# Rotary tables renewed by half sequence, weights in three turns, inverse norms on 128x32, and a new order of the slots

## The reference, cut to what matters

```
q, k, v = split(shift_tokens(x) @ Wqkv)           # 16 heads of 64
q = l2norm(q) * q_scale;  k = l2norm(k) * k_scale
q = q*cos*scale + rotate_half(q)*sin*scale        # k with 1/scale
o = softmax(q @ k.T * 8 over this and the previous window of 32) @ v
x = x + o @ Wo
xn = layernorm(shift_tokens(x)) * ln_g + ln_b     # the rows are shifted here too
a, gate = split(xn @ W1 + b1)
x = x + (a * gelu(gate)) @ W2 + b2
```

## Time and profile before

| | |
|---|---|
| median of three runs | 2486.25 us (2473.58, 2486.25, 2487.25) |
| the profiled execution | 2478.85 us, of which the span of its instructions 2477.0 |
| mean granted TensorE clock | 0.952 of full speed |
| PE, PEld | 2240.8 us busy (90%), 1255.8 (51%) |
| DVE | 1696.9 (69%) |
| POOL | 1463.3 (59%) |
| ACT | 1281.8 (52%) |
| DMA | 208.27 MB, mean 84 GB/s; queue of SP 32.4% of 16 engines |
| first and last norms of a front (L704) | 554.8 and 2369.8 us |

### The profile page before, as it was taken

One profiled execution on the slowest core, in us unless ns is written; L12 is line 12 of the kernel. 1 busy time (PEld: TensorE's weight loads), 2 busy tenths in 40 slices (PEclk: granted clock), 3 DMA queues, 4 the chain that ended last, 5 costly groups with the idle time before them and its releaser, 6 DMA issues. The chain is left out here.

```text
span 2477.0 us, 60119 instructions
## 1 busy us (share of the span) xinstructions
PE 2240.8 (90%) x23184; PEld 1255.8 (51%) x23184; DVE 1696.9 (69%) x3412; ACT 1281.8 (52%) x2402; POOL 1463.3 (59%) x1342
## 2 busy tenths in 40 slices
PE   8999999976889899998999989999899998999985
PEld 4545455533445455554555545555455554555542
DVE  5556555546767678776787767877668776787752
ACT  5565565632454455544555445554455544565442
POOL 3344433336666677666776667766666676676740
PEclk9999999987999999999999999999999999999997
DMA  1000000023343533445334353344534435344330
GB/s 56 6 1 5 1 5 1 1 65 96 90 114 99 145 89 97 114 100 143 88 96 114 101 143 89 96 113 102 143 88 105 112 93 143 95 101 110 93 86 21
DMA packets 219577, 208.27 MB, mean 84 GB/s; under 512 B 44194, under 2 KB 211104, under 8 KB 217760
## 3 DMA queue, kind: packets, MB, share of 16 engines
q1 hardware_dynamic: 219296, 204.45, 32.4%
HBM read 83.79 MB, written 13.63 MB: 39 GB/s over the span
## 5 line engine op out<-in xcount | busy, mean ns | idle before, releaser
L722 POOL TENSOR_TENSOR T<-T,RB 128x512 f32<-128x512 f32 x384 | 487.1, 1300 | 264.7 <-DMA RB<-norms 264.7
L647 PE MATMUL bank<-XT,WQK 128*128 128x256 f32 x1536 | 460.4, 426 | 155.6 <-DVE T L668 131.7
L673 POOL TENSOR_TENSOR T<-T 128x512 f32<-128x512 f32 x384 | 503.4, 1317 | 127.5 <-DVE T L668 127.4
L756 PE MATMUL bank<-WU,XT 128*32 128x512 f32 x3072 | 431.7, 635 | 1.7 <-ACT U L763 1.6
L647 PEld LDWEIGHTS bank<-XT,WQK 128*128 128x128 f32 x1536 | 278.1, 201 | 250.6 <-DVE T L668 151.7
L653 ACT ACTIVATE SQ<-bank 128x512 f32<-128x512 f32 x384 | 227.7, 593 | 296.0 <-PE bank L647 295.3
L413 POOL TENSOR_SCALAR PR<-PR,RI 128x512 f32<-128x512 f32 x256 | 173.9, 692 | 314.4 <-DVE RI L354 314.4
L763 ACT ACTIVATE U<-bank 128x512 f32<-128x512 f32 x384 | 229.3, 597 | 178.7 <-PE bank L853 140.3
L667 DVE TENSOR_TENSOR T<-bank,TAB 128x512 f32<-128x512 f32 x384 | 260.9, 679 | 83.0 <-ACT SQ L653 47.7
L349 DVE CUSTOM_DVE_ANT_0 PR<-bank,causal 128x512 f32<-128x512 f32 x256 | 174.3, 682 | 201.4 <-PE bank L192 201.3
L818 POOL TENSOR_TENSOR PL<-PL,RIL 128x512 f32<-128x512 f32 x192 | 201.3, 1048 | 143.9 <-DVE RIL L811 143.9
(11 more groups left out here) (110 smaller groups left out, 3463.3 us busy)
## 6 DMA issues: line engine op xcount, KB each, us to landing
RB<-norms SPq DMA_DIRECT2D x384, 128.0 KB, 3.1
KZ<-T SPq DMA_DIRECT2D x384, 128.0 KB, 2.6
QP<-T SPq DMA_DIRECT2D x192, 256.0 KB, 4.3
TAB<-rotary_dram SPq DMA_DIRECT2D x12, 1024.0 KB, 8.2
norms<-RN SPq DMA_DIRECT2D x96, 128.0 KB, 2.5
WQK<-wqk_halves_dram SPq DMA_DIRECT2D x12, 512.0 KB, 6.0
WVS<-wv_turned_dram SPq DMA_DIRECT2D x30, 128.0 KB, 2.5
WOS<-wo_lanes_dram SPq DMA_DIRECT2D x30, 128.0 KB, 2.7
```

What stands on the lines that cost most here:

```text
L647: m = pe.matmul(b[:, ab * HALF:(ab + 1) * HALF], WQK[:, kind, i, ab, :], XT[s % 2][:, hf * HALF:(hf + 1) * HALF], start=True, stop=True)
L673: pool.tensor_tensor(t1, t1, T2[i % 2][:, ::-1, :], ALU.add).then_inc(l_rotated.sem, 1)
L722: pool.tensor_tensor(t1, t1, RB[:, i:i + 1, :].to_broadcast([P, 2, HALF]), ALU.mult).then_inc(l_scaled.sem, 1)
L756: i = pe.matmul(bank[1][h * WIN:(h + 1) * WIN, :], XT[s % 2][:, c0:c0 + WIN], WU[:, lp * HG + h, :], start=True, stop=True)
```

## The change

- **Tables and weights.** WQK becomes three buffers of one kind each, taken in turn, so that the next layer's weights are loaded while the present ones are in use. The table is renewed in four parts (half sequence and kind), each as soon as the last products with that part are done, and folded in four parts by POOL.
- **Norms on 128x32.** ScalarE copies the square sums from PSUM to SS. SP gathers the meaningful rows by four DMAs into SM, 128x32, where every number counts. Clamp, guess and Newton step run on 128x32, and the store in DRAM is 16 KB for 128 KB. Norms in still reads four times into RB. `sp_norms` is cut in two, `sp_norms_out` and `sp_norms_in`.
- **Feed-forward rows** are scaled by ScalarE as rstd x + (-mean rstd); VectorE makes -mean and POOL the product.
- **Order.** All five slots are rewritten. In SP's slot the gather comes first, then the relayout; weight load, `sp_next_vo` and `sp_ffn_weights` stand between relayout and norms out; table load and `sp_shift` between norms out and norms in. On TensorE `values(k+1, 1)` stands late in slot k rather than early in the next, and `turn_probs` of half 0 at the slot's end. On POOL the four scalings stand first in the slot and the rotations of the next fronts behind them. On VectorE clamp and Newton step of a front are two entries with a product between them.

```diff
-            WQK = sbl('WQK', [P, 2, HG, 2, P])
+            WQK = [sbl(f'WQK{i}', [P, HG, 2, P]) for i in range(3)]
...
-            SM = sbl('SM', [P, HALF])
-            LG = sbl('LG', [P, HALF])
-            Y0 = sbl('Y0', [P, HALF])
-            Y2 = sbl('Y2', [P, HALF])
-            RN = sbl('RN', [P, HALF])
+            SS = sbl('SS', [P, HALF])
+            SM = sbl('SM', [P, WIN])
+            LG = sbl('LG', [P, WIN])
+            Y0 = sbl('Y0', [P, WIN])
+            Y2 = sbl('Y2', [P, WIN])
+            RN = sbl('RN', [P, WIN])
+            negm = sbl('negm', [P, TPB])
+            nmr = sbl('nmr', [P, TPB])
...
-            def sp_load_front(l, kind):
-                last = (l - 1) * 4 * BATCH + 14 + kind
+            def sp_load_weights(l, kind):
+                n = 2 * l + kind
+                if n >= 3:
+                    sp.wait_ge(l_front_done.sem, l_front_done.at((n - 3) // 2 * 16 + 14 + (n - 3) % 2))
+                sp.dma_start(WQK[n % 3][:, :, :, :], wqk[l, :, kind, :, :, :]).then_inc(s_wk[n % 3], 16)
+
+            def sp_load_table(l, part):
+                hf, kind = divmod(part, 2)
+                cols = slice(hf * HALF, (hf + 1) * HALF)
                 if l:
-                    sp.wait_ge(l_front_done.sem, l_front_done.at(last))
-                    sp.wait_ge(l_products.sem, l_products.at(last))
-                sp.dma_start(WQK[:, kind, :, :, :], wqk[l, :, kind, :, :, :]).then_inc(s_wk[kind], 16)
-                sp.dma_start(TAB[:, kind, :, :, :], rot[kind]).then_inc(s_wk[kind], 16)
-
-            def pool_fold_scale(l, kind):
-                pool.wait_ge(s_wk[kind], 32 * (l + 1))
+                    sp.wait_ge(l_products.sem, l_products.at((l - 1) * 16 + 12 + part))
+                sp.dma_start(TAB[:, kind, :, :, cols], rot[kind, :, :, :, cols]).then_inc(s_tb[part], 16)
+
+            def pool_fold_scale(l, part):
+                hf, kind = divmod(part, 2)
+                cols = slice(hf * HALF, (hf + 1) * HALF)
+                pool.wait_ge(s_tb[part], 16 * (l + 1))
                 for ab in range(2):
                     c = l * 4 + kind * 2 + ab
-                    i = pool.tensor_scalar(TAB[:, kind, :, ab, :], TAB[:, kind, :, ab, :], QSC[:, c:c + 1], 1.0, ALU.mult, ALU.mult)
+                    i = pool.tensor_scalar(TAB[:, kind, :, ab, cols], TAB[:, kind, :, ab, cols], QSC[:, c:c + 1], 1.0, ALU.mult, ALU.mult)
                 i.then_inc(l_folded.sem, 1)
...
-                pe.wait_ge(l_clamped.sem, l_clamped.at(f - 1))
+                pe.wait_ge(l_sums_kept.sem, l_sums_kept.at(f - 1))
...
+            def act_keep_sums(f):
+                act.wait_ge(l_sums_done.sem, l_sums_done.at(f))
+                act.wait_ge(s_sc, 64 * f)
+                act.activation(SS[:, :], bank[4][:, 0:HALF], ACT.Copy).then_inc(l_sums_kept.sem, 1)
+
+            def sp_gather_sums(f):
+                sp.wait_ge(l_sums_kept.sem, l_sums_kept.at(f))
+                sp.wait_ge(l_newton.sem, l_newton.at(f - 1))
+                for j in range(HG):
+                    r = slice(j * WIN, (j + 1) * WIN)
+                    sp.dma_start(SM[r, :], SS[j * WIN:j * WIN + HG, :].rearrange('h (t c) -> h t c', c=WIN)).then_inc(s_sc, 16)
+
             def dve_clamp(f):
-                dve.wait_ge(l_sums_done.sem, l_sums_done.at(f))
-                dve.wait_ge(l_newton.sem, l_newton.at(f - 1))
-                dve.wait_ge(l_guess.sem, l_guess.at(f - 1))
-                dve.tensor_scalar(SM[:, :], bank[4][:, 0:HALF], FAR, NORM2_EPS, ALU.min, ALU.max).then_inc(l_clamped.sem, 1)
+                dve.wait_ge(s_sc, 64 * (f + 1))
+                dve.tensor_scalar(SM[:, :], SM[:, :], FAR, NORM2_EPS, ALU.min, ALU.max).then_inc(l_clamped.sem, 1)
...
-            def sp_norms(f):
+            def sp_norms_out(f):
                 sp.wait_ge(l_newton.sem, l_newton.at(f))
                 if f >= 2:
                     sp.wait_ge(s_rb, 64 * (f - 1))
                 sp.dma_start(norms[f % 2], RN[:, :]).then_inc(s_rn, 16)
+
+            def sp_norms_in(f):
                 sp.wait_ge(s_rn, 16 * (f + 1))
                 sp.wait_ge(l_scaled.sem, l_scaled.at(f - 1))
-                rows = norms[f % 2].rearrange('(g h) (a c) -> h a g c', h=WIN, a=1)
+                rows = norms[f % 2].rearrange('(g h t a) c -> h a g (t c)', h=HG, t=8, a=1)
                 for h in range(HG):
                     sp.dma_start(RB[h * WIN:(h + 1) * WIN, :, :], rows[h].to_broadcast([WIN, HG, HALF])).then_inc(s_rb, 16)
...
+                dve.tensor_scalar(negm[:, :], mv[:, :, 0], -1.0, None, ALU.mult)
...
-            def dve_ffn_scale(s):
-                dve.wait_ge(f_rstd_done.sem, f_rstd_done.at(s))
-                dve.wait_ge(f_turned.sem, f_turned.at(s - 1))
+                pool.wait_ge(f_rstd_done.sem, f_rstd_done.at(s, 0))
+                pool.tensor_tensor(nmr[:, :], negm[:, :], rstd[:, :], ALU.mult).then_inc(f_rstd_done.sem, 1)
+
+            def act_ffn_scale(s):
+                act.wait_ge(f_rstd_done.sem, f_rstd_done.at(s))
+                act.wait_ge(f_turned.sem, f_turned.at(s - 1))
                 for t in range(TPB):
-                    i = dve.tensor_scalar(XN2[:, t, :], X2S[:, t, :], mv[:, t, 0:1], rstd[:, t:t + 1], ALU.subtract, ALU.mult)
+                    i = act.activation(XN2[:, t, :], X2S[:, t, :], ACT.Identity, scale=rstd[:, t:t + 1], bias=nmr[:, t:t + 1])
                 i.then_inc(f_scaled.sem, 1)
...
-            def change_at(v):
-                return v % 16 < 2 and 0 < v // 16 < DEPTH
+            def change_at(v, n):
+                return v % 16 < n and 0 < v // 16 < DEPTH
...
```

240 lines of the change are left out of this document (110 added, 130 removed).

## The result

| | before | after |
|---|---|---|
| median | 2483.38 us (2473.58 to 2487.25, 4 runs) | 2570.07 us (2568.90 to 2571.97, 4 runs) |
| ratio | | 1.0356, 95% interval 1.0323 to 1.0389 |
| profiled execution, span | 2478.85, 2477.0 | 2568.9, 2567.1 |
| granted TensorE clock | 0.952 | 0.953 |
| first and last norms in | 556.9, 2378.6 | 556.6, 2474.4 |

The change makes the kernel 3.6% slower, 87 us. The forecast was 2622 us, within 2530 to 2740. All of the loss lies between the first norms in and the last, 1821.7 us before and 1917.9 after (+96.2); what comes behind the last one takes 92.7 us for 98.4. In what follows a **round** is the time from the start of norms in of one front to that of the next.

A forecast was written before the change was run, and what follows sets the result against it. The SP-DMA-POOL loop was taken as the bound. From 2478.9 us, +5.3 us a step over 23 steps (+122) and +21 for layer changes gave 2622 us, range 2530 to 2740.

The forecast's parts named there:

- the loop: SP, DMA and POOL: norms in, RB lands, POOL scales, relayout, norms out lands, next norms in; about 18.5 us a round.
- shift ahead of norms in: SP queue, K front: a wait of 1.85 us becomes the shift's 8.1 us, +6.3 us a step.
- its old place: Shift behind norms in, in the kernel before: removing its cost, less later RB landing, gives -0.4 us a step.
- POOL late behind it: K front after the shift: POOL's scaling, late from VectorE's stall, is late no more, -0.5 us a step.
- `sp_next_vo`: SP queue, Q front: its two issues and 256 KB now stand ahead of norms out, +0.8 us a step.
- small norms: Norms out of 16 KB for 128 KB lands sooner: -0.3 us in three fronts, -0.9 us a step.
- The other steps: Layer changes, with weights, tables and feed-forward weights issued around norms out, plus the first layer's loads: +21 us in all.
- rival 3: SP queue: the gather comes into the loop and late sums hold the relayout; 2718 us or past 2900; chance 0.12.
- Row scaling on ScalarE: Feed-forward row scaling moved from VectorE into ScalarE's gaps, outside the loop: price 0.
- The gather: SP queue, beside RB's landing and POOL's scaling: four to five us of slack, so 0; upper bound about 1 us a front.
- Rival 1: VectorE's wait for X2S, not the loop, sets the period, so the change is faster: 2296 us; chance 0.10.
- Rival 2: The shift mostly hides, its third issue holding SP 1 us for 6.4: about 2490 us, no change; chance 0.08.

The follow-up runs named there:

- b_shift_between: Kernel before, with only the three X2S shift copies moved between norms out and norms in: 2586.95 us, ratio 1.0404 to the kernel before.
- a_shift_split: Changed kernel with the 127-partition shift copy cut into 112 and 15, its place kept: 2456.73 us, ratio 0.9880 to the kernel before.
- a_loads_behind: Changed kernel with next_vo, feed-forward weights, layer weights and table parts issued behind norms in, shift left in place: 2493.86 us, ratio 1.0042 to the kernel before.
- b_shift_split: Kernel before, with the 127-partition shift copy cut into 112 and 15: 2434.01 us, ratio 0.9791 to the kernel before.
- a_behind_b2: Changed kernel with the shift behind norms in and POOL's addition of b2 moved behind the four scalings: 2528.0 us, ratio 1.0185 to the kernel before.
- a_norms_full: Changed kernel with norms on 128x256 as before, no gather, norms out of 128 KB: 2636.9 us, ratio 1.0618 to the kernel before.
- a_dve_scale: Changed kernel with the feed-forward rows scaled by VectorE again: 2579.36 us, ratio 1.0390 to the kernel before.
- a_gather_twice: Changed kernel with the gather issued twice, first into a tile nothing reads: 2594.14 us, ratio 1.0452 to the kernel before.
- a_shift_behind: Changed kernel with the shift put behind norms in instead of ahead of it: 2621.58 us, ratio 1.0543 to the kernel before.

## Why the prediction was right, point by point

**The bound.** Right, and now shown. Issues put between two links of the loop lengthen the step, and issues taken out of it shorten it, in both kernels (b_shift_between, a_shift_split, a_loads_behind). The stall on VectorE that the trace of before shows most plainly was beside it: b_shift_split took VectorE's wait for X2S from 250.4 us to 122.3, 128 us less, and the time fell by 52. That holds for the order of the kernel before; with the shift behind norms in the stall enters the loop (a_behind_b2).

**The step, term by term.** An ordinary step is 77.9 - 75.6 = 2.3 us longer, for a forecast of 5.3; 23 of them make 54 us of the 96, for 122. Comparing a_norms_full with the kernel before leaves out the small norms, and comparing it with the kernel after gives them alone (from the means before rounding):

| term | forecast | measured | from |
|---|---|---|---|
| shift ahead of norms in | +6.3 | +6.2 | K (2), a_norms_full less before |
| its old place | -0.4 | -1.2 | Q (3), the same |
| POOL late behind it | -0.5 | -0.5 | K (0), the same |
| `sp_next_vo` | +0.8 | +0.9 | Q (1), the same; 1.0 by a_loads_behind |
| small norms | -0.9 | -3.1 | step, after less a_norms_full |
| sum | +5.3 | +2.3 | |

The step of the prediction that was mis-sized is "norms out of 16 KB for 128 KB ... I take -0.3 for the three fronts". It looked at one link, the landing of the store, and had that nearly right: 29.0 us over the whole span in a_norms_full less after, for 21. It left out two more links in which the same part of the change gains: the landing of RB (21.5 us) and POOL's scaling (15.1 us), which the prediction's "Price 0; it only moves slack" for the norm arithmetic had at nothing. Why RB lands sooner no run separates. In the ordinary steps this is 2.2 us too little, 50 us over 23 of them; the old place of the shift adds 18, and b_shift_split, which frees that round of the shift by another way, gives 1.2 us for it too. The Trainium skill (DMA: Bandwidth & Descriptors, Specifications) has transfers under 512 B read, modified and written; by that the small store would have gained nothing, and its rows of 128 B land 0.27 to 0.56 us sooner than those of 1 KB. The measurement decides.

**The other steps.** Forecast +21, measured 42: what the 23 steps leave of the 96 us. The feed-forward weights cost 5.8 us each for 3.0 (83.3 - 77.9 after, less 75.1 - 75.6 before). A layer change cost 8.2 us after for a forecast of 9.7, and 6.7 before for 9.1. So 68 us too much in ordinary steps and 21 too little in the others partly cancel, and the total of 2622 us is nearer to the measured 2570 than its parts are; that much of it is luck. The range is narrower than its own working, too: the gather's bound of 1 us a front isn't in it and stands only in rival 3.

**Priced at nothing.** Row scaling on ScalarE: within 0.9% (a_dve_scale). Norm arithmetic on 128x32: not nothing, 15 us by way of POOL. The gather: right that it costs nothing in the kernel after, as relayouts start when the scaling ends; wrong in its margin. "Four to five us of slack" is 1.5 us in one round of four (a_gather_twice). The order of POOL: in the kernel after `pool_ffn_b2` is done before RB lands, so it costs nothing there, but the prediction saw no wait in it, and the wait of `pool_ffn_b2` for X2S, ahead of the scaling, was the trap of a_shift_behind.

**The rivals.** Rival 1, that the stall is the bound, falls with b_shift_split and with the result. Rival 2, that the shift hides, falls with L916 itself, never under 6.47 us in 24 issues. Rival 3, the gather in the loop, did not happen here; its issues did stand in the loop in a_behind_b2 and a_gather_twice.

**The signs.** Eight us from norms out to norms in: 8.8. POOL idle 6 us longer: 10.8 for 4.5. TensorE idle ahead of the turned probabilities, under 90%: 85%. A step of about 80: 77.9 in the ordinary ones, 80.8 on average over all. The one that failed is VectorE, whose busy share fell by 6 points and not by 10, and whose wait for X2S was 155.7 us in 24 times for 250.4, shorter but not short. Its groups after (line, form, count, busy us, mean ns):

```profile
L725 DVE TENSOR_TENSOR Y<-Y 128x32 f32<-128x32 f32 x96 | 107.0, 1114 | 3.3
L728 DVE SCALAR_TENSOR_TENSOR RN<-Y 128x32 f32<-128x32 f32 x96 | 95.4, 994 | 3.3
L712 DVE TENSOR_SCALAR SM<-SM 128x32 f32<-128x32 f32 x96 | 64.9, 676 | 105.5 <-DMA SM<-SS 105.5
L723 DVE SCALAR_TENSOR_TENSOR Y<-SM,Y 128x32 f32<-128x32 f32 x96 | 43.5, 453 | 0.6 <-ACT Y L719 0.6
```

and those of before beside the earlier trace rows, with the row scaling of before:

```profile
L688 DVE TENSOR_SCALAR SM<-bank 128x256 f32<-128x256 f32 x96 | 40.3, 419 | 64.2 <-PE bank L681 64.2
...
L704 DVE SCALAR_TENSOR_TENSOR RN<-Y 128x256 f32<-128x256 f32 x96 | 78.2, 814 | 3.3
...
L921 DVE TENSOR_SCALAR XN<-X2S,mv,rstd 128x128 f32<-128x128 f32 x96 | 85.1, 945 | 1.4 <-POOL rstd L915 1.1 <-issue 0.2
```

The four instructions took 321.4 us on 128x256 (with 78.8 for L699 and 124.1 for L701) and take 310.8 on 128x32. An eighth of the columns saved 3% of VectorE's time. The 84 us that VectorE lost are nearly all the row scaling's 85.1. The timelines of VectorE and of POOL after show what such an instruction does with its time:

```profile
1077.23 1.16 DVE L725 TENSOR_TENSOR Y<-Y 128x32 f32<-128x32 f32 x1
1078.43 0.97 DVE L728 SCALAR_TENSOR_TENSOR RN<-Y 128x32 f32<-128x32 f32 x1
```

```profile
1077.05 1.29 POOL L748 TENSOR_TENSOR T<-T,RB 128x512 f32<-128x512 f32 x1
1078.30 1.04 POOL L844 TENSOR_TENSOR PL<-PL,RIL 128x512 f32<-128x512 f32 x1
```

L725 ends at 1078.39, 0.05 us after POOL's scaling; L728 at 1079.40, 0.06 us after POOL's normalising. This is the rule of the whole trace: all 96 L725 and 84 of the 96 L728 end within 0.12 us behind the end of a POOL instruction. The other twelve L728 have no POOL instruction beside them and take 0.191 to 0.193 us (median of all 1.186, most 1.204), and in a_behind_b2 21 of the 96 L725 take 0.19 us, as in the rows above, none of them with a POOL instruction beside it. So these instructions wait for POOL, and fewer columns can't shorten a wait. The Trainium skill (SBUF — State Buffer, section on SBUF's two sides) says just that: VectorE with two inputs in SBUF and POOL share a pair of ports, which one of them holds for its whole instruction. Here the trace agrees, and in both directions: on 128x256 the same arithmetic also held POOL (a_norms_full). "This takes VectorE's longest instruction ... down by most" was wrong for this reason; it did no harm to the forecast, as VectorE isn't in the loop. What the smaller arithmetic did give came through POOL, which is in the loop: 15.1 us, beside 50.5 from the transfers.

## What to carry to other kernels

Find the closed loop before pricing an edit: follow one front around the in-order queue that issues its DMAs, and ask of every issue whether it stands between two links of the loop or in the shadow of one. The same 8 us of issues lengthened their round by 1.2 us in one place of this queue and by 6.2 in another, and loads of a few hundred KB made up 76 us that another place in the queue gave back. And when an item is moved into the shadow, look for further ways into the loop: another engine's in-order queue where a consumer of it stands ahead of the loop's own work. Here there were two, on POOL and on VectorE.
